# A decoder with a delta-rule layer on one core: the block inverse on four 64x64 tiles, and all membranes stepped in the front stage

## What is computed

```python
mem = DECAY * mem + dt                      # DECAY 0.9, THR 0.5
spike = (mem > THR);  mem = mem - spike * THR
alpha = sigmoid(at + asp * spike);  beta = sigmoid(bt + sum(spike * bsp)) * active
s = s * alpha[..., None]
pred = einsum('bhk,bhkv->bhv', kt, s)
s = s + (beta * kt)[..., None] * (vt - pred)[:, :, None, :]
out = einsum('bhk,bhkv->bhv', qt, s)
```

## Time and profile before

| | |
|---|---|
| median of three runs | 2595.97 us |
| profiled execution, its own time | 2596.74 us |
| its span | 2594.9 us |
| front stage | 855.8 to 950.2 |
| delta stage | 950.2 to 2129.8 |
| first `diag` of groups 0 and 7 | 999.5 and 1965.9 |

### The profile page before, as it was taken

The page is one execution under the profiler, slowest core; times in us unless marked ns, Lnnn a source line. Parts: engine busy times, 40 slices in busy tenths (PEclk is TensorE's granted clock), DMA queues, the critical chain, the costliest instruction groups (busy, mean ns, idle before and its releaser), DMA issues. The chain is left out here.

```text
span 2594.9 us, 76890 instructions
## 1 busy us (share of the span) xinstructions
PE 2186.4 (84%) x32607; PEld 1506.7 (58%) x32607; DVE 1612.6 (62%) x4155; ACT 981.7 (38%) x1930; POOL 781.0 (30%) x884
## 2 busy tenths in 40 slices
PE   7999988999678658899999999999998968963774
PEld 4666656666556323656666666666666737652553
DVE  4766656666543675878686868778746422467444
ACT  3444444444223532343434343444443432312222
POOL 0111111111056713252432425152523210112773
PEclk9998989989589777899999999999998965555886
DMA  4000000000212220000000000000000011010114
GB/s 168 10 10 2 10 10 6 2 2 2 78 37 68 77 118 18 3 27 3 23 7 23 7 23 7 23 7 2 7 3 7 3 54 48 2 33 15 52 53 125
DMA packets 42516, 75.98 MB, mean 29 GB/s; under 512 B 5988, under 2 KB 27244, under 8 KB 39620
## 3 DMA queue, kind: packets, MB, share of 16 engines
q1 hardware_dynamic: 35140, 56.63, 6.4%
q0 software_dynamic: 7040, 14.43, 2.0%
HBM read 46.73 MB, written 24.31 MB: 27 GB/s over the span
## 5 line engine op out<-in xcount | busy, mean ns | idle before, releaser
L2786 DVE COPY_PREDICATED delta_neg_a_and_p_t<-delta_level_int,bank 128x256 f32<-128x256 uint8 x384 | 179.5, 537 | 65.6 <-PE bank L2293 65.0
L2317 PEld LDWEIGHTS bank<-delta_inverse,delta_neg_a_and_p_t 64*64 64x64 f32 x5120 | 171.4, 141 | 46.1 <-issue 45.6
L2317 PE MATMUL bank<-delta_inverse,delta_neg_a_and_p_t 64*64 64x64 f32 x5120 | 193.9, 228 | 0.0
L2690 POOL TENSOR_TENSOR delta_scaled_beta_k<-delta_scaled_beta_k,delta_decays 128x256 f32<-128x256 f32 x160 | 124.2, 776 | 223.4 <-issue 165.2
L2520 ACT ACTIVATE delta_two_less_ax<-bank 128x512 f32<-128x512 f32 x160 | 94.9, 597 | 243.0 <-PE bank L2317 241.6
L310 PE MATMUL bank<-attn_w_value_out,attn_z_self_t 128*64 128x512 f32 x512 | 144.7, 680 | 40.4 <-DVE attn_cross_attended_t L722 36.3
L699 POOL TENSOR_TENSOR attn_probs<-attn_probs,attn_row_sum 128x512 f32<-128x512 f32 x64 | 65.4, 1042 | 359.4 <-DVE attn_row_sum L781 359.4
L2293 PE MATMUL bank<-weights_sb,delta_scaled_beta_k 64*64 64x64 f32 x6144 | 128.7, 229 | 46.5 <-DVE delta_neg_a_and_p_t L2786 40.8
L2293 PEld LDWEIGHTS bank<-weights_sb,delta_scaled_beta_k 64*64 64x64 f32 x6144 | 110.2, 141 | 82.8 <-DVE delta_neg_a_and_p_t L2786 48.7
L601 ACT ACTIVATE attn_probs_t<-bank 128x512 f32<-128x512 f32 x128 | 71.3, 595 | 197.8 <-PE bank L409 197.8
L2339 PE MATMUL bank<-delta_two_less_ax,delta_inverse_t 64*64 64x64 f32 x4096 | 140.0, 224 | 5.2 <-issue 5.2
(11 more groups left out here) (545 smaller groups left out, 5021.3 us busy)
## 6 DMA issues: line engine op xcount, KB each, us to landing
delta_drives<-front_drive SPq DMA_DIRECT2D x7, 1024.0 KB, 3.8
weights_sb<-in_w_moe_dram SPq DMA_DIRECT2D x1, 4352.0 KB, 15.2
z_rows<-moe_z_all SPq DMA_DIRECT2D x16, 256.0 KB, 2.4
delta_odd_spikes<-delta_drives SPq DMA_DIRECT2D x4, 1024.0 KB, 4.9
weights_sb<-moe_outs SPq DMA_DIRECT2D x8, 512.0 KB, 7.4
weights_sb<-delta_drives SPq DMA_DIRECT2D x3, 1024.0 KB, 5.0
weights_sb<-in_w_delta_dram SPq DMA_DIRECT2D x1, 2816.0 KB, 9.4
weights_sb<-in_ctx_tok_dram SPq DMA_DIRECT2D x8, 264.0 KB, 5.9
```

Of the source, the lines that this page charges most:

```text
L2317: last = pe.matmul(out_[rows(sg), u], AP[rows(sg), hp, eo, b4, 0, :], X[rows(sg), hp, u], start=False, stop=True, skip_group_check=True)
L2690: pool.tensor_tensor(r_[:, :, 0, :], r_[:, :, 0, :], a_[:, :, 1, 0:1].to_broadcast([128, T // (2 * c), c]), ALU.mult)
L2786: last = dve.copy_predicated(second(AP[:, hp, eo, :, :, :].rearrange("p b i n -> p (b i) n"), c), m_, PAIR[hp % 2][eo][:, :].rearrange("p ...
```

## The change

Front stage: the drives of all eight groups are kept in SBUF with time outermost (`[128, S, NG, HDP, GB]`), and one pair of operations a time step does all groups, 128x256 elements, after the last drive. ScalarE's copy writes each drive with a step of 1024 bytes. `zr` is made by VectorE, for the groups one and two ahead of the convolution. The spikes are then compared group by group into bytes, over two buffers, and go to DRAM, 256 KB a group; group 0's go to the tile that the delta stage reads.

Delta stage: no membranes; SP loads the byte spikes, GpSimd turns them to fp32. `ax`, `xw` and `y` take four quadrants: `ax` from rows `sg` to the head's rows, so that W and the turned inverse `XT` stand in the head's rows, and `xw` from there to rows `sg`. The even sequences' part (`eo` 0) is turned straight, 128 rows at once; the odd one's crossed, two pieces of 64 rows. All of it goes by pairs of head pairs P (two banks of 512 columns); `INV` has banks 4, 5 for P = 0 and banks 2, 3 for P = 1, so from the fourth stage of products on both P share banks 0 and 1. The order on TensorE, ScalarE and VectorE is rewritten by P. Two casts in the attention stage that nothing reads are gone.

```diff
-                drive = sb("drive", [128, 4, HDP, T], ctx=ctx)
-                mem = sb("membrane", [128, 2 * HDP * GB], ctx=ctx)
+                drive = sb("drive", [128, S, NG, HDP, GB], ctx=ctx)
+                mem = sb("membrane", [128, NG * HDP * GB], ctx=ctx)
+                spk8 = sb("spike_bytes", [128, 2, S, HDP * GB], U8, ctx=ctx)
...
-                            act.activation(drive_of(g)[:, j, :], bank[4 + j][:, :], ACT.Copy, scale=2.0).then_inc(s["drive"], 1)
+                            act.activation(drive[:, :, g, j, :].rearrange("p t b -> p b t"), bank[4 + j][:, :].rearrange("p (b t) -> p b t", t=S),
+                                           ACT.Copy, scale=2.0).then_inc(s["drive"], 1)
...
                     def membrane(t):
-                        m_ = two[:, :, t]
+                        m_ = drive[:, t, :, :, :].rearrange("p g j b -> p (g j b)")
...
-                    dve.wait_ge(s["drive"], 2 * HDP)
-                    for g in range(4, NG):
-                        for t in range(6 * (g - 4), 6 * (g - 3)):
-                            membrane(t)
-                        conv(g)
-                    for t in range(6 * (NG - 4), S):
+                    dve.wait_ge(s["drive"], NG * HDP)
+                    for t in range(S):
                         membrane(t)
+                    dve.tensor_scalar(spk0.rearrange("p j (b t) -> p (j b) t", t=S), drive_of(0).rearrange("p t n -> p n t"), 1.0, None, ALU.is_gt).then_inc(s["spikes"], 1)
+                    for g in range(1, NG):
+                        if g >= 3:
+                            dve.wait_ge(spikes_out[g % 2], 16 * ((g - 1) // 2))
+                        dve.tensor_scalar(spk8[:, g % 2, :, :], drive_of(g), 1.0, None, ALU.is_gt).then_inc(s["spikes"], 1)
...
+                INV = ((bank[4], bank[5]), (bank[2], bank[3]))
+                OUT = ((bank[0], bank[1]), (bank[4], bank[5]))
+                STRAIGHT_AND_CROSSED = ((0, slice(0, 128), slice(0, 128)), (1, slice(0, 64), slice(64, 128)), (1, slice(64, 128), slice(0, 64)))
+                def product_banks(stage_, P):
+                    return PAIR[P if stage_ < 3 else 0]
...
+                    def ax(g, l, P):
+                        if l > 1:
+                            pe.wait_ge(s["x"], 16 * g + 4 * (l - 2) + 2 * P + 2)
+                        elif P == 0:
+                            if g >= 1:
+                                pe.wait_ge(s["o_read"], 4 * g)
+                        else:
+                            pe.wait_ge(s["masked"], 14 * g + 2 * 2 + 2)
+                        for eo in range(2):
+                            for sg in range(2):
+                                pe.matmul(INV[P][eo][rows(sg ^ eo), :], identb[rows(sg), rows(sg)],
+                                          eye2b[rows(sg), :].unsqueeze(1).to_broadcast([64, 8, 64]), start=True, stop=False,
+                                          skip_group_check=True)
...
+                        for hp, b, eo, b4, par, r, sg, u, first in units(P):
+                            last = pe.matmul(INV[P][eo][r, u], AP[rows(sg), eo, hp, b4, 0, :], X[rows(sg), eo, hp, b4 * 64:b4 * 64 + 64],
+                                             start=False, stop=True, skip_group_check=True)
...
+                    def turned(g, l, P):
+                        for eo, to, of in STRAIGHT_AND_CROSSED:
+                            dve.wait_ge(s["x"], 16 * g + 4 * (l - 1) + 2 * P + eo + 1)
+                            last = dve.transpose(XT[to, eo, hps(P), :].rearrange("p h n -> p (h n)"),
+                                                 X[of, eo, hps(P), :].rearrange("p h n -> p (h n)"))
+                        last.then_inc(s["x_t"], 1)
```

More of the change, by code:

```diff
@@ new lines, in diag @@
+                    def diag(g, P):
+                        two = product_banks_free(g, 0, P)
+                        pe.wait_ge(s["kr_rd"], nth_of("kr", g, 2 * P + 1))
+                        pe.wait_ge(s["q_rd"], nth_of("q", g, 2 * P + 1))
+                        for hp, b, eo, b4, par, r, sg, u, first in units(P):
+                            t = slice(b * S, b * S + S)
+                            last = pe.matmul(two[eo][rows(sg), u], kr[r, hp, t], kq[r, g % 2, 1, hp, t],
+                                             start=first, stop=True, skip_group_check=True)
+                        last.then_inc(s["products"], 1)
@@ new lines, in products @@
+                    def products(g, l, P):
+                        c = 1 << l
+                        two = product_banks_free(g, l + 1, P)
+                        pe.wait_ge(s["scaled_kq"], 24 * g + HDP * l + 2 * P + 2)
+                        if l > 0:
+                            pe.wait_ge(s["scaled_kr"], 20 * g + HDP * (l - 1) + 2 * P + 2)
+                        for hp, b, eo, b4, par, r, sg, u, first in units(P):
+                            t = slice(b * S, b * S + S)
+                            last = pe.matmul(two[eo][rows(sg), u], kr[r, hp, t], second(kq[r, g % 2, :, hp, t], c),
+                                             start=first, stop=True, skip_group_check=True)
+                        last.then_inc(s["products"], 1)
@@ L2345, in values @@
+                    def values(g, half):
+                        if half == 0:
+                            pe.wait_ge(s["masked"], 14 * (g + 1))
+                        else:
+                            pe.wait_ge(s["v"], 4 * g + 2)
+                        for b2 in range(2):
+                            b4 = 2 * half + b2
                             for eo in range(2):
@@ L2995, in _ @@
                             f_bk(it + 1)
-                        if drive:
-                            membrane(it + 2, 26, 40)
+                        if core:
+                            masked(it, 6, 0)
+                            turned(it, 4, 0)
                         if tail:
@@ L3000, in _ @@
                         if core:
[L3001 to L3004 removed]
+                            masked(it, 6, 1)
+                            turned(it, 4, 1)
                         if tail:
```

584 lines of the change are left out of this document (265 added, 319 removed).

## The result

The change makes the kernel slower, by 0.9%: little, but clear of the noise. Median 2618.06 us (2608.3 to 2633.0, twelve runs) against 2594.99 (2588.5 to 2597.9, twelve runs); the ratio is 1.0093, 95% interval 1.0078 to 1.0108. The forecast was 2460, range 2400 to 2535. The profiled execution took 2608.45 with a span of 2606.5.

What follows compares the result with a forecast made beforehand. The prediction took TensorE's queue to bound the delta loop, and VectorE the front stage once the drives are there. 2596.7 - 185 (delta loop) + 50 (front) - 0.8 (casts) = 2460.9, forecast 2460 us, range 2400 to 2535.

Steps and rivals of the forecast that it cites:

- TensorE's work: Delta loop: four quadrants for ax (-13.5), xw (-8.0) and y (-1.8), with +1.6 for splits, sum -21.7 us a group.
- +1.6 for three splits: Delta loop, TensorE: three more changes between full array and quadrants, +0.5 us each, +1.6 a group.
- The casts: End of the attention stage: two casts go, -0.8 us.
- The front stage: All drives needed before the first membrane step, then steps and comparisons: stage ends near 1001.5, +50 us (bounds +38 to +75).
- VectorE's work: Delta loop: membranes go, masked copies merge (-2), third transpose piece and additions (+7.6): about 81 us of a group.
- New waits on TensorE ... net about +4: Delta loop: waits at t_ss, ax(1, 1), products(2, 1), f_al(2), t_ff(1) and f_bk, less waits paid today: about +4 us.
- The sum itself: Inner group of the delta loop: 135.4 - 21.7 + 4 - 1 = 116.7, taken as 116 us.
- 2388: Rival 3: cover better than the hand schedule, copies free, 108 us a group, front +42: 2388 us, chance 0.14.
- Membranes off VectorE, -4.9: Delta loop: membrane operations leave VectorE's queue, -4.9 us in each of six groups.
- Rival 1: VectorE paces the delta loop, 1.3 us wait in each of eight half levels, +10 a group: 2540 us, chance 0.12.
- Rivals 2 and 5: 2: copies out of PSUM pace the loop, 2516, chance 0.08; 5: accumulating matmuls don't overlap in four quadrants, 2686, 0.04.
- Rival 4: Front stage dearer, at its upper bound: 2485 us, chance 0.12.

Runs made afterwards that it cites:

- the dummies: Ten bf16 matmuls put between diag and t_ss, in the changed kernel with t_gated, t_hidden, f_bk and x(3, 0) moved: 0.9725 of the kernel before.
- the mended order: Changed kernel with t_gated, t_hidden, f_bk(0, 1) and x_out(3, 0) earlier, o(1) ahead of f_kr(3), log table loaded between the u copies: 0.9653 of the kernel before.

## Why the prediction was wrong

- **TensorE's work**: right. -21.7 forecast, -23.5 by the sum of block prices. Inside it, `xw` gains 0.9 in four of five levels and nothing in the fifth (-6.8 by these prices where I had -8.0), and the split `values` take 4.8 us (2.9 and 1.9, the first partly at the lower clock) where in one piece they took 3.6; I had them among +1.6 for three splits.
- **The casts**: right. -0.8 forecast; from the start of the last addition of the attention stage to the next stage it is 2.58 before (677.13 to 679.71) and 1.81 after (678.69 to 680.50). The addition itself came 1.6 later, so the stage's end doesn't show it.
- **The front stage**: right in the total, +46 for +50, in part by luck. The copies were too cheap in my sum and their +5 on the stage was too much: all drives were there 66 us after the stage's start, where I had 71, so the copies are hidden behind other work. The membrane steps take 0.42 at a spacing of 0.46 and start at 923.09 (forecast 926). The drive copies are dearer than my 0.95 and lie at the upper bound; the comparisons wait 0.9 for each pair of transfers:

```profile
L1948 ACT ACTIVATE front_drive<-bank 128x512 f32<-128x512 f32 x32 | 29.3, 1079 | 0.0
...
981.04 1.90 DVE L2017 TENSOR_SCALAR weights_sb<-front_drive 128x2048 f32<-128x2048 f32 x1
982.86 2.35 DVE L2021 TENSOR_SCALAR front_spike_bytes<-front_drive 128x2048 uint8<-128x2048 f32 x2
986.12 2.36 DVE L2021 TENSOR_SCALAR front_spike_bytes<-front_drive 128x2048 uint8<-128x2048 f32 x2 [0.91 <-DMA delta_spikes<-front_spike_bytes]
```

  The copy went from 0.60 to 1.08. The prediction's estimate of about 1.0, worked out from the rule of cachelines in the Trainium skill, "SBUF — State Buffer", is near it: this case's 1.08 agrees with the rule for ScalarE too, which no row of before could show.
- **VectorE's work**: the size was off, 87 to 88 us a group for 81. The masked copies gained more than I had: one of 128x512 takes 0.914 in the mean, two of 256 took 0.537 each, 0.16 less in a pair for my 0.07. But the additions of `first_inverse` take 1.06 (128 rows) and 1.28 (64 rows) where 0.68 was the row, and a transpose 0.70 for 0.62. By the lines of the seventh group, before and after, additions and transposes cost 12.1 more, for my 7.6:

```profile
L2827 DVE TENSOR_TENSOR delta_inverse_t<-delta_neg_a_and_p_t,delta_two_eye 64x512 f32<-64x512 f32 x4 | 5.1, 1276 | 0.1
...
L2827 DVE TENSOR_TENSOR delta_inverse_t<-delta_neg_a_and_p_t,delta_two_eye 128x512 f32<-128x512 f32 x2 | 2.1, 1063 | 0.0
```

- **"New waits on TensorE ... net about +4"**: this is the step that failed. Measured +21 a group (15.6 to 36.7), with the gain from the membranes already taken off. The five inner groups have 109 of the 151 us that are missing in the delta stage (137.9 where 116 was forecast), the seventh 15, the first 7; the last (111.8 where 94 was forecast) has another 18, at a granted clock of 0.82. The three places, mended, gave back 110 us (1.0068 to 0.9653). I found the place at `t_ss` and one at `t_ff(1)` and `f_bk`, and priced them at +1.6 and +3, by the wait alone. The place behind `t_gated` I didn't see, nor the pauses inside blocks (+4.0 a group). And no wait had the half clock behind it in my sum, though the earlier trace rows showed it for before (3.74 us of wait, then 64 loads in 3.32 instead of 1.95). At `t_ss`, 1.75 us of wait were followed by 20 us of half clock; the dummies alone gave back 36 us in seven groups, 5 a group.
- **The sum itself**: 135.4 - 21.7 + 4 - 1 takes off 1 us that the text doesn't give; the wait of 1.0 at products(0, 2) is already in the net 4, so it is most likely counted twice. With 116 for 116.7 that makes 1.7 a group, some 10 us in all. The front's 950.2 to 1001.5 is 51 and not 50, and the range of 2400 to 2535 leaves out two of the rivals that it is said to cover (2388 and 2540). None of this is near the 151.
- **Membranes off VectorE, -4.9**: 3.0 to 3.6 in that order.
- **Rival 1** (VectorE paces the loop, 2540) was nearest in cause: its waits are for VectorE. It looked for them at the masked copies, and they were at the fills' banks; with `t_gated` moved, 4 us a group of them did come at the masked copies. What is left of the difference in the mended order (122 for 116) isn't settled: that rival, the wait for `f_beta`'s rows (2.7) and the pauses inside blocks (2.5) are all in it. **Rivals 2 and 5** are out: no wait for ScalarE's copies of W and X is among the large ones, and the tiles overlap (`ax` 1.11). **Rival 4** is out with the front at +46.
- The chances were the second error. A schedule followed over 87 + 55 + 52 us of other engines' work, in an order that is new on three of them, carried 0.95 for faster. The mechanism with a loss on the far side was not the overlap of the tiles; it was the order.

## What to carry over

When a change rewrites the order around the bound engine, go through every point at which it takes a buffer that another engine empties, and write down what stands ahead of that emptying in the other's queue; price each with the slow clock that follows. To learn whether such waits come of the engine's new speed or of the order, take the speed back alone and look at the same waits: here they stayed as they were. Where the time doesn't come, look first at such single operations: five moves gave 4% here, with the same work. A part that takes load from an engine (the membranes) is worth only what that engine's place in the order makes it worth: 18, 47 and some 60 us in three orders of one kernel.

## What the runs showed of the hardware

- A wait of 1.75 us at the start of a group was followed by 20 us of the lower granted clock (in other groups of the same kernel waits of 2.4 and 2.5 there by 10), one of 4.5 us by 6.8 and one of 3.8 by 13.7. The length of the slow stretch doesn't follow the wait's. Ten dummy matmuls of bf16 (1.84 us) in the first removed it altogether.
- With `ax`, `xw` and `y` back on two quadrants the inner groups ran at 0.91 instead of 0.88: less work for TensorE went with a lower clock.
- With `ax`, `xw` and `y` on four quadrants, 64 loads and 64 matmuls of fp32 go out in about 1.1 us, and TensorE pauses inside blocks for 4.7 us a group, each pause ending 1.2 to 1.5 us after a 16 KB instruction transfer; on two quadrants it pauses 0.1.
- Two transposes or additions of 64 rows on different halves of the partitions don't overlap on VectorE: three pieces take 2.15 us, as three whole ones would (0.71 each).
- With 28 us of small operations more in VectorE's queue, the masked copy behind them made TensorE wait up to 6.5 us, and the granted clock of the inner groups fell from 0.88 to 0.84:

```profile
PEld bank L2293 <- DVE delta_neg_a_and_p_t L2796: 31.3, 6, 6.5
```
